# Selective scan between two mixers: one group's product with C moved from VectorE to GpSimd

## What is computed

```python
def step(h, inp):
    u_t, d_t, B_t, C_t = inp
    dA = jnp.exp(d_t[..., None] * As)
    h = h * dA + (d_t * u_t)[..., None] * B_t[:, :, None, :]
    y = jnp.einsum('bkcn,bkn->bkc', h, C_t)
    return (h, y)
```

## Time and profile before

| | |
|---|---|
| median of 3 runs | 3185.19 us |
| the profiled execution | 3182.6 us, its span 3180.7 us |
| main loop | from about 1017 to 3146 us: 64 stages, 768 groups |
| busy over the span | PE 87%, DVE 82%, POOL 68%, ACT 57% |
| granted TensorE clock | 0.992 over the span, 1.00 in the stages below |

### The profile page before, as it was taken

The page is one execution under the profiler, slowest core; times in us unless marked ns, Lnnn a source line. Parts: engine busy times, 40 slices in busy tenths (PEclk is TensorE's granted clock), DMA queues, the critical chain, the costliest instruction groups (busy, mean ns, idle before and its releaser), DMA issues.

```text
span 3180.7 us, 101339 instructions
## 1 busy us (share of the span) xinstructions
PE 2769.5 (87%) x39496; PEld 2066.3 (65%) x39496; DVE 2619.2 (82%) x4161; ACT 1824.7 (57%) x3872; POOL 2154.2 (68%) x1814
## 2 busy tenths in 40 slices
PE   4999999999996788888888888888888888888886
PEld 4999999996664555656656566565665655656554
DVE  6444444445776999999999999999999999999995
ACT  1111111112224777777777777777777777777773
POOL 5333333330004988889888888888988888888883
PEclk9999999999997999999999999999999999999999
DMA  5000000002334554554545545455455554555541
GB/s 203 0 0 0 0 0 0 0 0 88 114 112 138 155 163 151 160 177 141 172 147 163 173 143 169 152 166 167 144 169 157 163 164 146 165 164 159 168 144 48
DMA packets 57086, 385.30 MB, mean 121 GB/s; under 512 B 10100, under 2 KB 15060, under 8 KB 31700
## 3 DMA queue, kind: packets, MB, share of 16 engines
q1 hardware_dynamic: 57044, 384.79, 39.2%
HBM read 352.64 MB, written 32.11 MB: 121 GB/s over the span
## 4 chain that ended last, share of the span: by engine, by line
POOL 34%; issue 30%; PE 25%; DVE 7%; ACT 2%; DMA 1%; POOLq 1%; SPq 0%; ACTq 0%; DVEq 0%
POOL arena L489 21%; PE ps L1096 10%; PE ps L1105 9%; POOL arena L462 3%; POOL arena L471 3%; POOL arena L476 3%; POOL arena L466 3%; PE ps L1092 2%; DVE arena L769 2%; DVE conv_out L201 2%; DVE arena L772 1%; DMA x_in<-x_pair 1%; POOL arena L454 1%; POOL arena L449 1%; DVE stats L565 1%
## 5 line engine op out<-in xcount | busy, mean ns | idle before, releaser
L1228 PE MATMUL ps<-arena,ident 128*128 128x392 f32 (+1 forms) x4096 | 1162.4, 416 | 0.9 <-DVE arena L781 0.9
L947 ACT ACTIVATE ps<-arena,abias,a 128x390 f32<-128x390 f32 x1024 | 691.3, 677 | 320.8 <-DVE arena L772 181.9
L781 DVE TENSOR_TENSOR arena<-arena,ps 128x784 f32<-128x784 f32 x768 | 745.8, 971 | 38.3 <-PE ps L1218 13.0
L1228 PEld LDWEIGHTS ps<-arena,ident 128*128 128x128 f32 x4096 | 682.1, 191 | 144.3 <-issue 1.3
L769 DVE TENSOR_TENSOR_SCAN arena<-ps,arena 128x392 f32<-128x392 f32 x768 | 703.2, 957 | 16.9 <-POOL arena L489 15.7
L772 DVE TENSOR_TENSOR_SCAN arena<-ps,arena 128x392 f32<-128x392 f32 x768 | 703.2, 957 | 0.0
L1218 PE MATMUL ps<-arena,sel 96*128 96x196 bf16 x3072 | 391.4, 250 | 307.7 <-DVE arena L781 307.7
L1218 PEld LDWEIGHTS ps<-arena,sel 96*128 96x128 bf16 x3072 | 227.4, 97 | 610.7 <-DVE arena L781 575.8
L951 ACT ACTIVATE ps<-arena,abias,a 128x195 f32<-128x195 f32 x1024 | 477.6, 504 | 198.4 <-DVE arena L769 107.0
L489 POOL TENSOR_TENSOR arena<-arena 128x784 f32<-128x784 f32 x256 | 473.2, 1851 | 148.8 <-PE ps L1228 146.4
L489 POOL TENSOR_TENSOR arena<-arena,wh_sb 128x784 f32<-128x784 f32 x256 | 471.7, 1848 | 64.0 <-PE ps L1228 61.0
(11 more groups left out here) (172 smaller groups left out, 3136.1 us busy)
## 6 DMA issues: line engine op xcount, KB each, us to landing
wx_sb<-b_by_state SPq DMA_DIRECT2D x64, 1568.0 KB, 6.3
wh_sb<-b_by_state SPq DMA_DIRECT2D x64, 1568.0 KB, 6.2
arena<-b_by_image SPq DMA_DIRECT2D x128, 784.0 KB, 9.0
arena<-x_seq SPq DMA_DIRECT2D x4, 2352.0 KB, 15.9
x_in<-x_pair SPq DMA_DIRECT2D x16, 588.0 KB, 4.3
x_dram<-x SPq DMA_DIRECT2D x16, 588.0 KB, 2.8
x<-x_dram SPq DMA_DIRECT2D x16, 588.0 KB, 10.0
out<-xhat SPq DMA_DIRECT2D x16, 588.0 KB, 2.8
```

What stands on the lines that cost most here:

```text
L781: dve.tensor_tensor(h, h, bank(3), ALU.mult).then_inc(s["readout_ready"], 1)
L947: ins = act.activation(r, src, ACT.Exp, scale=a01[:, c:c + 1], bias=abias01[:, c:c + 1])
L1228: mm = pe.matmul(ps[:, 5 if g < 8 else 6, 0:cols], ident[:, :], h[:, m * cols:(m + 1) * cols], start=(opens and m == 0), stop=(closes and ...
```

## The change

The read-out of group 3 of each stage is done by POOL (`pool_read`) instead of DVE. POOL takes C from SBUF (`c_chunk`, rows of C spread by a DMA, as B is), after drive 6. DVE's read-out of group 2 and PE's spread for it add 2 instead of 1 to their counters. At step 3 PE issues the spread of group 4, at step 4 none. The reduction of group 3 stands at step 6 behind that of group 5, and waits for POOL; so the order of reductions is 0, 1, 2, 4, 5, 3, 6, ... and the drives' waits count in it. PE work for the pair before moves one step later where it stood at steps 3, 4 (stages 0, 1, 3), 5 and 6.

```diff
+POOL_READS = (3,)
+READ_LEAD = 3
+BEHIND = 2
...
+                for q, g in enumerate(POOL_READS):
+                    for img in range(2):
+                        sp.dma_start(c_by_state[k][q, :, img, :], xdbl[N * img + 2 * g:N * img + 2 * g + 2, T:T2]
+                                     ).then_inc(s["c_spilled"], 16)
...
+            def spread_c(P, k, first=False):
+
+                sp.wait_ge(s["c_spilled"], (P + 1) * (32 * len(POOL_READS)))
+                if not first:
+                    sp.wait_ge(s["pool_read"], P * len(POOL_READS))
+                rows = c_by_state[k].rearrange("q n i t -> (q n i t)").unsqueeze(0)
+                sp.dma_start(c_chunk[:, :], rows.broadcast_to([128, len(POOL_READS) * GC])).then_inc(s["c_chunk_in"], 16)
...
+                    if ahead and max(POOL_READS) + READ_LEAD < 8:
+                        spread_c(P1, k1)
                     if ahead:
                         spread_b(P1, k1, 1)
...
-                    pool.wait_ge(s["reduced"], G - (RING - 1))
+                    before = st * GRP + g - RING
+                    place = before // GRP * GRP + ORDER.index(before % GRP)
+                    pool.wait_ge(s["reduced"], G - (st * GRP + g) + (place + 1))
...
+            def pool_read(P, st, g, G):
+
+                _, _, view = group_aps(g)
+                h = view(hb[(st * GRP + g) % RING])
+                q = POOL_READS.index(g)
+                if q == 0:
+                    pool.wait_ge(s["c_chunk_in"], P * 16 + 16)
+                pool.wait_ge(s["scan_done"], G * 2 + 2)
+                pool.tensor_tensor(h, h, view(c_chunk[:, q * GC:(q + 1) * GC]), ALU.mult).then_inc(s["pool_read"], 1)
...
                         drive(P, st, g, i * (K4 * GRP) + (st * GRP + g), head and st * GRP + g < RING)
+                        if g - READ_LEAD in POOL_READS:
+                            pool_read(P, st, g - READ_LEAD, i * (K4 * GRP) + (st * GRP + (g - READ_LEAD)))
...
-                        read_out(st, g, G)
+                        if g not in POOL_READS:
+                            read_out(st, g, G)
...
-                            if (st, g) in ((2, 8), (3, 5), (3, 7)):
-                                result(i - 1, {8: 0, 5: 1, 7: 2}[g])
+                            if (st, g) in ((2, 8), (3, 6), (3, 8)):
+                                result(i - 1, (g // 2 - 2) if st == 3 else 0)
...
-                        spread(g, st)
-                        if not opening:
+                        if g in POOL_READS:
+                            spread(g + 1, st)
+                        elif g - 1 not in POOL_READS:
+                            spread(g, st)
+                        if not opening and (g - 1) % GRP not in POOL_READS:
...
                             reduce(*((st, g - 1) if g else ((st - 1) % K4, GRP - 1)))
+                        if g - 1 - BEHIND in POOL_READS:
+                            r = g - 1 - BEHIND
+                            pe.wait_ge(s["pool_read"], P * len(POOL_READS) + (POOL_READS.index(r) + 1))
+                            reduce(st, r)
...
-                            if (st, g) == (0, 3):
+                            if (st, g) == (0, 4):
                                 centre_hw(i - 1)
-                            if (st, g) == (0, 4):
+                            if (st, g) == (0, 5):
                                 centre_wh()
-                            if (st, g) == (0, 6):
+                            if (st, g) == (0, 7):
                                 centre_rest(i - 1)
-                            if (st, g) in ((1, 4), (1, 6)):
+                            if (st, g) in ((1, 5), (1, 7)):
                                 var(i - 1, g // 2 - 2)
-                            if (st, g) in ((2, 6), (3, 3), (3, 5)):
+                            if (st, g) in ((2, 6), (3, 4), (3, 6)):
```

More of the change, by code:

```diff
@@ L54, in build @@
     b_by_image = nc.dram_tensor("b_by_image", [K4, 2, N, T], F32)
+    c_by_state = nc.dram_tensor("c_by_state", [K4, len(POOL_READS), 2, 2, T], F32)
     with ExitStack() as ctx:
@@ L75, in build @@
         ident = sb("ident", [128, 128])
+        c_chunk = sb("c_chunk", [128, len(POOL_READS) * GC])
         sel = sb("sel", [96, N, 3, 128], BF16)
@@ L184, in build @@
             "oproj_ready", "o_ready", "out_stored", "fin_z", "fin_x1",
-            "b_spilled", "b_chunk0", "b_chunk1", "b_chunk2", "skipped")}
+            "b_spilled", "b_chunk0", "b_chunk1", "b_chunk2", "skipped",
+            "c_spilled", "c_chunk_in", "pool_read")}
         convs = ((pad01, conv01_out, 2 * H + 1, par01, s["conv01_step"]), (pad2, conv2_out, H, par2, s["conv2_step"]))
@@ L215, in group_aps, with reduce_order @@
                     lambda a: a.rearrange("p (m q t) -> p m q t", m=2, q=2))
+        def reduce_order():
+            order, late = [], []
+            for g in range(GRP):
+                if g in POOL_READS:
+                    late.append(g)
+                else:
+                    order.append(g)
+                order += [r for r in late if r + BEHIND == g]
+            return order
+        ORDER = reduce_order()
         def half_cols(hf):
@@ L318, in _ @@
                 spread_b(0, 0, j, True)
+            spread_c(0, 0, True)
             spill_xc(PAIRS - 1)
@@ L347, in pair @@
                         next_x(i)
+                    if ahead and max(POOL_READS) + READ_LEAD < 8:
+                        spread_c(P1, k1)
                     if ahead:
                         spread_b(P1, k1, 1)
+                    if ahead and max(POOL_READS) + READ_LEAD >= 8:
+                        spread_c(P1, k1)
                     if st == 3 and not head:
@@ L780, in read_out @@
                 dve.wait_ge(s["c_ready"], G + 1)
-                dve.tensor_tensor(h, h, bank(3), ALU.mult).then_inc(s["readout_ready"], 1)
+                dve.tensor_tensor(h, h, bank(3), ALU.mult).then_inc(s["readout_ready"], 1 + (g + 1 in POOL_READS))
             def pair(i, head, last):
@@ L902, in read_bc @@
                     act.wait_ge(s["b_spilled"], P * 48)
+                    act.wait_ge(s["c_spilled"], P * (32 * len(POOL_READS)))
                 act.activation(xdbl[:, :], ps[:, 7, 0:T2], ACT.Copy).then_inc(s["xdbl_ready"], 1)
@@ L1218, in spread @@
                     mm = pe.matmul(ps[:, 3 + m // 2, m % 2 * T:m % 2 * T + T], sel[:, n, kind, :], rhs, start=True, stop=True)
-                mm.then_inc(s["c_ready"], 1)
+                mm.then_inc(s["c_ready"], 1 + (g + 1 in POOL_READS))
             def reduce(st, g):
@@ L1225, in reduce @@
                 cols = GC // runs
-                opens, closes = st % 2 == 0 and g in (0, 8), st % 2 == 1 and g in (7, 11)
+                tile = [r for r in ORDER if (r < 8) == (g < 8)]
+                opens, closes = st % 2 == 0 and g == tile[0], st % 2 == 1 and g == tile[-1]
                 for m in range(runs):
@@ L1310, in pair @@
                         if not head:
-                            if g in (3, 4) and ahead:
-                                if st != 3 or g == 3:
-                                    pe.wait_ge(s["dt_read"], P1 * 4 + 4)
-                            if (st, g) == (0, 3):
+                            if (st, g) in ((0, 4), (1, 5), (2, 6), (3, 4)) and ahead:
+                                pe.wait_ge(s["dt_read"], P1 * 4 + 4)
+                            if (st, g) == (0, 4):
                                 centre_hw(i - 1)
-                            if (st, g) == (0, 4):
+                            if (st, g) == (0, 5):
                                 centre_wh()
-                            if (st, g) == (0, 6):
+                            if (st, g) == (0, 7):
                                 centre_rest(i - 1)
-                            if (st, g) in ((1, 4), (1, 6)):
+                            if (st, g) in ((1, 5), (1, 7)):
                                 var(i - 1, g // 2 - 2)
-                            if (st, g) in ((2, 6), (3, 3), (3, 5)):
-                                out_proj(i - 1, {6: 0, 3: 1, 5: 2}[g])
-                                residual(i - 1, {6: 0, 3: 1, 5: 2}[g])
+                            if (st, g) in ((2, 6), (3, 4), (3, 6)):
+                                out_proj(i - 1, (g // 2 - 1) if st == 3 else 0)
+                                residual(i - 1, (g // 2 - 1) if st == 3 else 0)
                         if g in (8, 9) and not (last and st >= 2):
```

## The result

The changed kernel takes 3249.31 us (median of 4 runs, 3247.55 to 3251.56) against 3184.8 before (median of 4 runs timed beside it; the 3185.19 ahead is of 3): ratio 1.0206, 95% interval 1.0194 to 1.0219, **64.5 us slower**. The forecast was 3204, range 3177 to 3222: the sign was right, the size not, by 45 us.

The account below looks back on a forecast made before the run. DVE bounds the kernel; after the change POOL bounds the stage border. Pair 134.46 against 133.08, +1.38; fifteen pairs +20.7, first pair -2.3, together +18.4 on 3182.6, 3201.0; median 2.6 above: 3204 us, range 3177 to 3222.

Parts of the forecast that it names:

- Removed read-out: DVE, group 3 of each stage: costs 1.74 instead of 2.755 us, 1.01 less; a stage limited only by DVE takes 32.05.
- the drain rule: DVE's paired scans: next operation starts only when the pipeline is empty, so the pair takes 1.93; some 12 us in all, 3216.
- pool_read: POOL's read-out of group 3, behind drive 6: takes 1.85 us, starts at about 11.3; up to 1.3 us more costs nothing.
- POOL's border: Stage end: drive 9 waits for reduction 3, so the next stage starts no sooner than 32.49, or 32.75 from stages 0 and 1.
- The norm wait: Stage 2: normed behind drive 4 ends at 8.55, ACT's affine and decays wait, DVE stalls 2.38 us at scan 4.
- centre_rest: Stage 0, PE after step 7: makes read-out 8 about 0.35 us late, covered by a POOL wait of 0.70 at stage end.
- out_proj behind two reductions: Step 6 of stages 2 and 3: PE's two reductions plus out_proj delay read-out 7, a new DVE stall of 1.24 us.
- the price of PE's step 5 and 6 in stages 1 and 2: PE durations assumed behind the empty step 4: spread 0.34 us, reduction 1.34 to the next instruction, 1.51 to its end.
- The port: Rival, chance 0.03: an in-place POOL operation holds DVE for its 1.85 us, 64 times, 118 us: 3322 us.
- Pair 0: First pair, without affine and out_proj: four stages of 32.49 instead of 33.06, -2.3 us.

Follow-up runs that it names:

- BEHIND = 1: Changed kernel with reduction 3 at step 5, one step earlier, behind that of group 4: 3169.3 us, ratio to before 0.9956.
- normed moved: Changed kernel with normed behind drive 1 instead of drive 4 of stage 2: 3193.94 us, 55.4 less.

## Why the prediction was wrong, step by step

- **Removed read-out: right.** Two scans 0.87 apart; four scans in a row take 3.56 us (1.83 + 2 x 0.87 = 3.57). The pure DVE stage was seen at 32.06. By the drain rule that the prediction took from the Trainium skill (VectorE: DVE Perf Modes, "The DRAIN you can't avoid") it would have been 0.19 longer; the trace disagrees. The same section excepts a next operation that is not held, which starts earlier; the prediction left the exception out.

```profile
1540.21 3.56 DVE L823 TENSOR_TENSOR_SCAN arena<-ps,arena 128x392 f32<-128x392 f32 x4
```

- **pool_read: right.** Median 1.85 us, at 11.2 into the stage (1609.12); drive 9 not held by it.

```profile
L548 POOL TENSOR_TENSOR arena<-arena,c_chunk x55: 1826/1854/1879, 1268.9 to 3121.2; 128x784 f32<-128x784 f32 x55
```

- **POOL's border: right where TensorE is at its higher clock.** 32.85 against 32.75 in stage 0, and 32.85 in stage 1 with the gap filled.
- **The norm wait: right.** 1.87 + 0.25 = 2.12 us of DVE stall, forecast 2.38, and ACT waits the 3 us that it named; normed starts 7.04 into the stage (1639.33), forecast 7.13.
- **centre_rest: right**, read-out 8 of stage 0 is 0.35 late, and POOL's border covers it.

```profile
1588.34 0.97 DVE L832 TENSOR_TENSOR arena<-arena,ps 128x784 f32<-128x784 f32 x1 [0.35 <-PE ps L1271]
```

- **out_proj behind two reductions: right in stage 3** (33.20 against 33.29; read-out 7 waits 1.15, forecast 1.24), in stage 2 1.76 instead of 1.24, for the next reason.
- **The step that failed: the price of PE's step 5 and 6 in stages 1 and 2**, "spread takes 0.34 and a reduction 1.34". Those rows were taken from a TensorE that had hardly rested: the longest wait of its matmuls for DVE was 1.0 us. I counted the empty step 4 as a relief alone and never asked what its 2.6 us do to what follows. At the lower clock spread and reduction 4 cost 0.63 + 2.52 (1610.89 to 1614.04), not 1.68, in this pair, and more in others. Against the forecast, stage 1 is 2.01 us longer in the mean and stage 2 0.93, 2.94 a pair, 44 us in fifteen pairs. The forecast for the profiled execution was 3201.0 and it took 3250.7, so these 44 are nearly all of the 49.7 us; the rest is the loop's later start (4.9, last point) and pair 0 (0.5). The range didn't hold the time because every bound in it was a duration at the higher clock.

```profile
PE ps L1218 <- DVE arena L781: 259.0, 376, 1.0
...
PE ps L1271 <- DVE arena L832: 287.7, 290, 5.4
```

  These two lines of the waits from 1240 to 3150 us, of before and of after, are who waited for whom (us in total, times, longest): it was to be seen in the timeline of before that no such idle stretch existed there, so the price behind one had no row.
- **The port: no.** Scans last 946 to 975 ns, as before, with POOL's product beside them; the warning of the Trainium skill that the prediction weighed (Perfetto Trace Analysis, "Optimizing Scalar/DVE Operations"), that such a move might not help, is not borne out for these instructions.

```profile
L820 DVE TENSOR_TENSOR_SCAN arena<-ps,arena x663: 946/949/975, 1239.2 to 3149.9; 128x392 f32<-128x392 f32 x166
```

- Pair 0 gained 1.8 us, forecast 2.3. The loop starts 4.9 us later than before (first scan at 1022.65, not 1017.74), which was not forecast. In the ten experiments it starts between 1017.89 and 1022.67 with the same work ahead of it, so it is not laid to the change; its cause is not known.

## What to carry to other kernels

Taking work from the bound engine pays only as far as the handed-over piece returns in time: here one place in the order of reductions (step 6 or step 5) was worth 80 us, more than the 64.5 that the change had lost. When work is taken out of TensorE's list, look at what the hole does to the matmuls behind it; an empty step can cost more than the step did, and real work that may stand anywhere belongs there. And a helper engine's lead is a stock that other engines draw on: list all who wait for it (here affine, by way of normed) before it is spent.

## What the runs showed of the hardware that I had not expected

- After 2.62 us without work TensorE's granted clock went from 1.00 to 0.51, and matmuls ran at 1.2 GHz for about 3 us in one pair (1610.89 to 1614.04) and for 6 in another (1884.14 to 1890.04), whose stage 1 took 35.93. In the kernel before, the clock was 1.00 from 1026 us to 3163 us, all but the ends of the loop. Useless matmuls of 1.94 us in the gap took 21 us off the kernel, and 24 with `BEHIND = 1` and var moved.
- The same idle stretch is not always followed by the fall. Of 14 pairs the clock fell behind the 2.62 us of stage 1 in 14 (the changed kernel), 10 (`BEHIND = 1`) and 3 (normed moved), and within one kernel a fall made the stage 1.7 us longer (34.21 for 32.52). With `BEHIND = 1` the length of the gap and the list of work ahead of it are the same in the pairs that fell and in those that didn't, so neither alone decides. What does stays open.
